# Second-choice expert rows: half the transposing loads replaced by TensorE transposes, and a reordered GpSimd queue, in a linear-attention and mixture-of-experts layer

## The chip, the cores and the metric

One Trainium2 chip, 8 NeuronCores. Each core works on one of the 8 sequences of the batch; the cores exchange nothing. The metric is the device time of the slowest core in microseconds (us). Each core has TensorE (matmul), VectorE, ScalarE, GpSimd and SyncE; SyncE and GpSimd issue the DMAs of this kernel, and 16 DMA engines carry them.

## What is computed

For every core one sequence x of 4096 tokens by 1024 features, weights shared:

```
q = elu(x Wq^T + bq) + 1;  k = elu(x Wk^T + bk) + 1;  v = x Wv^T + bv      (16 heads of 64)
attention: causal linear attention in chunks of 128 tokens, state S += k^T v, out = num / den
x1  = layernorm(x + out Wo^T + bo)
gates = softmax(x1 gate_w^T + gate_b) over 8 experts; the two largest are kept
ffn = sum over the two chosen experts e of gate_e * (x1 expert_w[e]^T + expert_b[e])
out = layernorm(x1 + ffn)
```

## The kernel before, in words

The attention runs over 32 chunks of 128 tokens in a software pipeline that is written out by hand (the loop at L771). For each chunk it ends with the first layer norm, the gate and the top-2 choice, and then `stage_scatter` (L686) sends each token's row to two lists in HBM by an indirect DMA of GpSimd: to `xs` in bf16 at its place in the list of its second choice, and to `xfd` in f32 at its place in the list of its first choice. The index of the token is stored in the row itself. Expert weights are converted to bf16 in HBM during the attention and loaded into the eight tensors W0 to W7 as these come free (`load_experts`, L752); experts 3 and 7 come last, since W3 holds Wo and W7 the attention tiles.

Each list is cut into tiles of 128 rows that belong to one expert: NT = 39 tiles. The first eight are the first tiles of the eight experts, at fixed places; the others' places and weights are read from a table (`tab`) computed after the last chunk, by register loads (`at_row` L922, `value` L911).

**Stage 1, second choices (loop at L1014).** For a tile t, `load_second` (L977) issues two DMAs on SyncE's queue: a transposing DMA that brings 128 rows of `xs` as the transposed stationary operand into one of six buffers `xTb`, and a small DMA for the 128 token indices `tk`. It is called AHEAD = 5 tiles early. `expert_mm` (L936) is 16 matmuls of 128x128 by 512 on TensorE into one of four pairs of PSUM banks. ScalarE copies the result to Y (L1022), and GpSimd scatters it to `y2d` (helper line L206). VectorE does nothing in this stage.

**Stage 2, first choices (loop at L1084).** Six tiles ahead, SyncE loads the f32 rows of `xfd` (L1001); the buffer must have been written out by the scatter to `out` (`xf_out`). Three tiles ahead, GpSimd gathers the tokens' rows of `y2d` (helper line L212). ScalarE casts the rows to bf16 (L1048), TensorE transposes them in 8 steps and the gate columns in one (L1058, L1056), ScalarE copies the transposed rows from PSUM (L1063), VectorE copies the gate columns (L1066). After two matmuls for the bias (L954) and 16 for the expert (L960), VectorE adds the gathered rows (L1107), adds the gated PSUM result (L1111), and computes mean and variance (L1117, L1121). GpSimd makes the scale and shift by three small operations, the "norm" below (L1123, L1126, L1129), ScalarE applies them (L1096) and GpSimd scatters the rows to `out` (`put_out`, L206). GpSimd's order in round t is: gather of tile t+3, output of tile t-1, norm of tile t. Every engine and each DMA queue works in the order in which the program issues.

## Time and profile before

| what | us |
|---|---|
| median of 3 runs (lowest to highest) | 1058.51 (1056.54 to 1061.42) |
| the profiled execution, whole | 1057.53 |
| its span on the slowest core, core 6 | 1056.0 |
| spans of the eight cores | 1041.1 to 1056.0 |
| PE / DVE / ACT / POOL busy on core 6 | 908.1 / 576.9 / 540.7 / 431.5 |
| HBM traffic of core 6 over the span | 227 GB/s |

The span is divided as follows on core 6: the attention until about 646 us, stage 1 from 655.72 to about 835 us, stage 2 until the end. PE is TensorE's matmul row, PEld its weight load, DVE is VectorE, ACT ScalarE, POOL GpSimd, SPq the DMA issues of SyncE. A busy share is an average over stages; what bounds a stage is read from its waits. Times in the rows below count from the first instruction of the core that they name.

### The profile page before, as it was taken

Reading aid. Unit: us, or ns where it says so; the run is one execution under the profiler, and the core shown is the slowest. Engines: PE = TensorE matmul, PEld = TensorE weight load, DVE = VectorE, ACT = ScalarE, POOL = GpSimd, SP = SyncE. Lnnn points to the kernel's source line nnn. Section 1 sums busy time; section 2 is a strip of 40 time slices with the busy share of each in tenths; the row PEclk is TensorE's granted clock in tenths of the full one; section 3 lists DMA queues with packets and bytes.
Section 4 is the critical chain, followed back from the end, with each engine's and each line's share of the span. In section 5 each row is a group of like instructions: output and inputs, shape, how many; then the busy total and the mean of one; then the engine's idle time right before and its main releaser. Section 6 shows DMA issues by size and latency. Waiting matters only on the chain.

```text
span 1056.0 us, 21222 instructions; the slowest of 8 cores (1041.1 to 1056.0 us)
## 1 busy us (share of the span) xinstructions
PE 908.1 (86%) x6495; PEld 457.0 (43%) x6606; DVE 576.9 (55%) x1243; ACT 540.7 (51%) x731; POOL 431.5 (41%) x674
## 2 busy tenths in 40 slices
PE   4799899999998999999999863579778899999992
PEld 1344454555544545554555541234333344444441
DVE  4345766766666667666667764000000088888883
ACT  0663665756657566566656541112112455666552
POOL 9101433534434334325232424313222356777763
PEclk9899999999999999999999986889989899999997
DMA  9989796977976967868537995989999768987861
GB/s 139 160 156 314 138 209 143 177 156 149 180 155 130 189 150 137 189 126 157 137 106 226 285 294 180 296 160 235 182 168 255 203 210 277 309 267 249 304 208 58
DMA packets 126490, 204.96 MB, mean 194 GB/s; under 512 B 59422, under 2 KB 73886, under 8 KB 126384
## 3 DMA queue, kind: packets, MB, share of 16 engines
q0 software_dynamic: 53808, 130.92, 54.9%
q1 hardware_dynamic: 72576, 72.69, 26.3%
q8 instruction: 59, 0.97, 0.4%
q14 instruction: 47, 0.39, 0.1%
HBM read 142.93 MB, written 97.21 MB: 227 GB/s over the span
## 4 chain that ended last, share of the span: by engine, by line
PE 52%; ACT 11%; issue 10%; DMA 8%; POOL 7%; DVE 7%; SPq 3%; DVEq 0%; ACTq 0%; POOLq 0%
PE PS L309 20%; PE PS L960 13%; PE PS L547 10%; ACT AR L325 4%; DMA AR<-xs 4%; POOL out L206 3%; ACT AR L326 3%; DMA W<-wq 2%; SPq L983 2%; PE PS L467 1%; PE PS L593 1%; PE PS L461 1%; POOL rstd L1126 1%; DMA y2d<-AR,ix 1%; PE PS L502 1%
## 5 line engine op out<-in xcount | busy, mean ns | idle before, releaser
L309 PE MATMUL PS<-W 128*128 128x512 bf16 x1474 | 347.9, 384 | 33.6 <-DVE acc L266 15.0
L960 PE MATMUL PS<-W,AR 128*128 (+1 forms) x1215 | 285.3, 391 | 46.1 <-DMA AR<-xs 40.3
L309 PEld LDWEIGHTS PS<-W 128*128 128x128 bf16 x1536 | 143.7, 99 | 192.4 <-issue 38.4
L960 PEld LDWEIGHTS PS<-W,AR 128*128 128x128 bf16 x1248 | 121.6, 100 | 208.3 <-issue 80.8
L330 DVE SCALAR_TENSOR_TENSOR W<-AR 128x512 bf16<-128x512 f32 x128 | 88.5, 692 | 140.6 <-ACT AR L326 125.3
L325 ACT ACTIVATE AR<-PS,cbs 128x512 f32<-128x512 f32 x128 | 87.9, 687 | 87.8 <-PE PS L309 82.6
L547 PE MATMUL PS<-W 128*128 128x512 bf16 x496 | 115.2, 386 | 6.5 <-DVE ixf L637 3.2
L1022 ACT ACTIVATE AR<-PS 128x1024 f32<-128x1024 f32 x39 | 39.8, 1023 | 152.2 <-PE PS L960 147.3
L1066 DVE COPY wT<-PS 16x128 bf16<-16x128 bf16 x39 | 7.3, 188 | 186.5 <-PE PS L1058 186.0
L206 POOL DMA_INDIRECT xs<-AR x32 | 34.5, 1078 | 181.4 <-DVE rden L479 143.0
L1096 ACT ACTIVATE AR<-AR,nmr,rstd 128x1024 f32<-128x1024 f32 x39 | 48.4, 1241 | 80.4 <-POOL nmr L1129 80.4
L206 POOL DMA_INDIRECT y2d<-AR,ix x39 | 37.6, 963 | 125.0 <-ACT AR L1022 110.4
L326 ACT ACTIVATE AR<-PS,cbs 128x512 f32<-128x512 f32 x128 | 87.7, 685 | 0.0
L438 DVE TENSOR_TENSOR W<-PS,cbs 128x1024 bf16<-128x1024 f32 x64 | 75.1, 1215 | 0.1
L547 PEld LDWEIGHTS PS<-W 128*128 128x128 bf16 x512 | 48.3, 99 | 60.6 <-issue 8.1
L518 ACT ACTIVATE AR<-S_f 64x520 bf16<-64x520 f32 x62 | 39.8, 642 | 51.1 <-DVE S_f L509 46.6
L206 POOL DMA_INDIRECT out<-AR x39 | 53.1, 1360 | 30.2 <-issue 9.9
L565 POOL TENSOR_TENSOR rstd<-mnv,epst 128x1 f32<-128x1 f32 x32 | 6.2, 194 | 137.5 <-DVE mnv L563 120.4
L1111 DVE SCALAR_TENSOR_TENSOR AR<-PS,AR 128x1024 f32<-128x1024 f32 x39 | 50.1, 1284 | 21.3 <-PE PS L960 20.9
L402 POOL DMA_DIRECT2D AR<-x x32 | 32.3, 1046 | 67.6 <-DMA AR<-AR 67.3
L1117 DVE BATCH_NORM_STATS2 lnst<-AR 128x6 f32<-128x512 f32 x78 | 50.2, 685 | 6.5 <-DVE AR L1111 6.2
L1107 DVE SCALAR_TENSOR_TENSOR AR<-AR 128x1024 f32<-128x1024 f32 x39 | 50.1, 1285 | 4.7 <-DMA AR<-y2d,AR 3.6
(123 smaller groups left out, 1265.4 us busy)
## 6 DMA issues: line engine op xcount, KB each, us to landing
AR<-xfd SPq DMA_DIRECT2D x39, 524.0 KB
AR<-AR SPq DMA_DIRECT2D x32, 512.0 KB, 5.8
AR<-x POOLq DMA_DIRECT2D x32, 512.0 KB, 7.2
escr<-ew POOLq DMA_DIRECT2D x64, 256.0 KB
W<-escr SPq DMA_DIRECT2D x40, 256.0 KB, 5.1
W<-xt POOLq DMA_DIRECT2D x64, 128.0 KB, 12.7
W<-escr SPq DMA_DIRECT2D x48, 128.0 KB
xfd<-AR SPq DMA_DIRECT2D x9, 524.0 KB, 6.2
```

Of the source, the lines that this page charges most:

```text
L206: return Q.op("POOL", lambda e: e.indirect_dma_start(out=out, out_offset=bass.IndirectOffsetOnAxis(ap=idx, axis=0), in_=in_, in_offset=Non ...
L309: return Q.op("PE", lambda e: e.matmul(bank(b), lt, rh, start=(k == 0), stop=(k == KB - 1)), inc="cpe" if k == KB - 1 else None)
L325: Q.op("ACT", lambda e: e.activation(e1, bank(b), AF.Exp, bias=bc), inc="cac")
L326: va = Q.op("ACT", lambda e: e.activation(e2, bank(b), AF.Relu, bias=bc), inc="cac")
L330: vd = Q.op("DVE", lambda e: e.scalar_tensor_tensor(dst, e1, 1.0, e2, ALU.min, ALU.add), inc="cdv")
L438: msc_tok[j][hf] = Q.op("DVE", lambda e, hf=hf: e.tensor_tensor(msc[j][hf].rearrange("p (h w) -> p h w", w=128), PS[:, hf * 1024:(hf + 1) ...
L547: vpe = Q.op("PE", lambda e, b=b, k=k, hh=hh: e.matmul(bank(b), attnT[j][:, k * 128:(k + 1) * 128], wcol(3, k, hh * 512, 512), start=(k == ...
L960: mm = e.matmul(bank(2 * pi + hh), xTb[i][:, k * 128:(k + 1) * 128], w, start=(lst == 1 and k == 0), stop=(k == KB - 1))
L1096: vo = Q.op("ACT", lambda e, x=x, val=val: e.activation(val, val, AF.Identity, bias=nmr[x][:, 0:1], scale=rstd[x][:, 0:1]), inc="cac")
L1107: v1 = Q.op("DVE", lambda e, i=i, j=j, val=val: e.scalar_tensor_tensor(val, Y[j], XF[i][:, F_GATE + 1:F_GATE + 2], val, ALU.mult, ALU.add) ...
L1111: v2 = Q.op("DVE", lambda e, i=i, pi=pi, val=val: e.scalar_tensor_tensor(val, PS[:, pi * 1024:(pi + 1) * 1024], XF[i][:, F_GATE:F_GATE + 1 ...
L1117: vb = Q.op("DVE", lambda e, i=i, x=x, hh=hh: e.bn_stats(lnst[x][:, hh * 6:(hh + 1) * 6], XF[i][:, hh * 512:(hh + 1) * 512]), inc="cdv")
```

## The change

1. `load_second` has two forms. For the first eight tiles and then for every even one (24 of 39) it issues one plain DMA of 128 whole rows of `xs`, the token index with them, into one of six row buffers R; no `tk` load is needed. Four of these lie in XF[6] and XF[7], two in xb. The 15 odd tiles keep the transposing DMA and the `tk` load.
2. `turn_second` transposes such a tile on TensorE (8 transposes into PSUM bank 6 or 7), and VectorE copies it to `xTb`. In round t it stands for tile t+1 ahead of the matmuls of tile t, and `load_second(t + 5)` now stands ahead of both. `expert_mm` uses three PSUM pairs, not four.
3. A plain load waits for `r_free` of its row buffer, which holds the transposes and the scatter to `y2d` of the tile before in it.
4. The weights of experts 3 and 7 (16 DMAs of 256 KB) are issued as soon as the last output projection has ended, ahead of the first five tile loads, not behind them.
5. In stage 2 the gate-column copy moves from VectorE to ScalarE, and GpSimd's order in round t becomes: norm of tile t, output of tile t-1, gather of tile t+3.
6. A row of `xs` shrinks from 1056 to 1040 elements (BW).

```diff
+    R = [XF[6 + j // 2].bitcast(BF16)[:, j % 2 * BW:(j % 2 + 1) * BW] for j in range(4)] + xb
@@ load_experts
+        if g == NCH:
+            Q.wait("SP", attnT_free[(NCH - 1) % 2])
+            for e_i in (3, 7):
+                load_w(e_i)
@@ stage 1
+    turned = lambda t: t < 8 or t % 2 == 0
+    tb, nturn = [bfree[6], bfree[7]], [0]
     def load_second(t):
-        i = ring_of(t, 1)
-        Q.wait("SP", *xT_free[i])
+        i, n = ring_of(t, 1), t % len(R)
         if t >= 8:
             Q.wait("SP", v_tab, v_padn)
+        if turned(t):
+            Q.wait("SP", *r_free[n], *(dsf if n > 3 else []))
+            r_tok[t] = Q.op("SP", lambda e: at_row(
+                e, t, 1, BW, 2, lambda rows: e.dma_start(R[n], xs[rows, :])),
+                inc=f"dr{n}", k=16)
+            return
+        Q.wait("SP", *xT_free[i])
...
+    def turn_second(t):
+        i, n, b = ring_of(t, 1), t % len(R), nturn[0] % 2
+        nturn[0] += 1
+        Q.wait("PE", r_tok[t], *tb[b])
+        for k in range(KB):
+            vpe = Q.op("PE", lambda e, k=k: e.transpose(
+                bankb(6 + b)[:, k * 128:(k + 1) * 128], R[n][:, k * 128:(k + 1) * 128], Id),
+                inc="cpe" if k == KB - 1 else None)
+        r_free[n] = [vpe]
+        Q.wait("DVE", vpe, *xT_free[i])
+        xT_tok[(t, 1)] = Q.op("DVE", lambda e: e.tensor_copy(xTb[i], bankb(6 + b)),
+                              inc="cdv")
+        tb[b] = [xT_tok[(t, 1)]]
...
     for t in range(AHEAD):
         load_second(t)
-    for e_i in (3, 7):
-        load_w(e_i)
...
+    turn_second(0)
     for t in range(NT):
-        pi, i = t % 4, t % NY
-        vpe = expert_mm(t, 1, pi)
+        pi, i, n = t % 3, t % NY, t % len(R)
         if t + AHEAD < NT:
             load_second(t + AHEAD)
         if t >= 12 and t % 4 == 0 and (t - 12) // 4 < AHEADF:
             load_first((t - 12) // 4)
+        if t + 1 < NT and turned(t + 1):
+            turn_second(t + 1)
+        vpe = expert_mm(t, 1, pi)
...
+        (r_free if turned(t) else tk_free)[n].append(y2_tok[i])
@@ stage 2
-        Q.wait("DVE", vpe, *xT_free[ring_of(t - 2, 0)])
-        wT_tok[t] = Q.op("DVE", lambda e: e.tensor_copy(
-            wT[j][:], bankb(7)[0:16, 0:128]), inc="cdv")
+        Q.wait("ACT", *xT_free[ring_of(t - 2, 0)])
+        wT_tok[t] = Q.op("ACT", lambda e: e.activation(
+            wT[j][:], bankb(7)[0:16, 0:128], AF.Copy), inc="cac")
@@ loop of stage 2, head
-        if t + 3 < NT:
-            gather_y2(t + 3)
...
-            put_out(t - 1, vo)
-        if t == NT:
+        if t == NT:
+            put_out(t - 1, vo)
             break
@@ loop of stage 2, after the norm of tile t
+        if t > 0:
+            put_out(t - 1, vo)
+        if t + 3 < NT:
+            gather_y2(t + 3)
```

## Rows read from the trace of the kernel before

**Rows 1.** Spans and mean granted TensorE clock, two of the eight cores.
```profile
core 3: 1042.0 us, clock 0.963
...
core 6: 1056.0 us, clock 0.959
```
**Rows 2.** Windows, core 6: stretch, length, busy time per engine, PEclk, DMA share, GB/s.
```profile
740.00:796.00 56.00, 41.51 (x159) 17.01 (x163) 0.00 (x0) 10.52 (x11) 13.45 (x14) 0.90 1.17 178
```
**Rows 3.** Timeline, core 6, PE, stage 1: start, length, operation, [idle before and releaser].
```profile
655.72 18.63 PE L960 MATMUL PS<-W,AR 128*128 128x512 bf16 x78 [9.34 <-DMA AR<-xs]
692.07 47.04 PE L960 MATMUL PS<-W,AR 128*128 128x512 bf16 x204 [17.71 <-DMA AR<-xs]
...
796.84 38.34 PE L960 MATMUL PS<-W,AR 128*128 x170 [0.22 <-issue]
```
**Rows 4.** Timeline, core 6: SyncE's DMA issues of the last weights.
```profile
661.80 9.22 SPq L194 DMA_DIRECT2D W<-escr  x16
```
**Rows 5.** The chain that ended last, core 6, in order of time: start, length, what.
```profile
647.86 3.60 DMA xs<-AR
...
671.06 20.73 DMA AR<-xs
...
746.61 11.19 DMA y2d<-AR,ix
```
**Rows 6.** DMA, core 6: all queues over 600 to 636, then over 636 to 652 us.
```profile
DMA packets 8106, 10.72 MB, mean 298 GB/s; under 512 B 931, under 2 KB 6358, under 8 KB 8102
...
DMA packets 1342, 3.04 MB, mean 190 GB/s; under 512 B 171, under 2 KB 768, under 8 KB 1339
```
**Rows 7.** SyncE's queue over 600-636, 692-716, 768-796 us: packets, MB, share of 16 engines.
```profile
q1 hardware_dynamic: 7256, 7.66, 73.2%
...
q1 hardware_dynamic: 8702, 1.87, 48.1%
...
q1 hardware_dynamic: 6170, 2.04, 81.8%
```
**Rows 8.** Lines L417 and L1066, core 6: copies from PSUM, duration in ns min/median/max.
```profile
L417 DVE COPY AR<-PS x32: 682/691/692, 73.5 to 617.8; 128x1024 bf16<-128x1024 bf16 x32
...
L1066 DVE COPY wT<-PS x39: 184/185/213, 838.3 to 1031.2; 16x128 bf16<-16x128 bf16 x39
```
**Rows 9.** Timeline, core 6, one round of stage 2.
```profile
855.35 0.21 DVE L1121 BATCH_NORM_AGGREGATE mnv<-lnst 128x2 f32<-128x12 f32 x1
...
855.69 1.28 DVE L1107 SCALAR_TENSOR_TENSOR AR<-AR 128x1024 f32<-128x1024 f32 x1
856.25 0.76 POOL L1123 TENSOR_TENSOR rstd<-mnv,epst 128x1 f32<-128x1 f32 x1
...
857.28 0.62 PE L1058 MATMUL PS<-id_b,AR 128*128 128x128 bf16 x8
857.37 1.28 DVE L1111 SCALAR_TENSOR_TENSOR AR<-PS,AR 128x1024 f32<-128x1024 f32 x1 [0.40 <-PE PS L960]
...
858.60 1.09 POOL L212 DMA_INDIRECT AR<-y2d,AR  x1 [0.44 <-issue]
...
860.15 0.21 DVE L1121 BATCH_NORM_AGGREGATE mnv<-lnst 128x2 f32<-128x12 f32 x1
```
**Rows 10.** Timeline, core 6, GpSimd in another round: an output that lasts longer.
```profile
914.38 2.07 POOL L206 DMA_INDIRECT out<-AR  x1 [0.31 <-DVE wT L1066]
```
**Rows 11.** Line L212 on core 3: gathers of y2d, from issue to landing.
```profile
DMA to landing us min/median/max: 2.2/7.3/9.4
```
**Rows 12.** Timeline, core 6, PE: first and last matmuls of stage 2.
```profile
841.72 1.89 PE L960 MATMUL PS<-W,AR 128*128 128x512 bf16 x4
...
1033.56 3.63 PE L960 MATMUL PS<-W,AR 128*128 x15
```
**Rows 13.** Timeline, core 3, PE: first and last matmuls of stage 2.
```profile
835.19 4.96 PE L960 MATMUL PS<-W,AR 128*128 128x512 bf16 x16
...
1020.54 3.63 PE L960 MATMUL PS<-W,AR 128*128 x16
```

More of the change, by code:

```diff
@@ L29 @@
 F_TOK, F_POS, F_GATE = 1040, 1041, 1043
-BW = 1056
+BW = 1040
 OOB = 1 << 20
@@ L111, in build @@
     attnT = [wcol(7, 6 + j, 0, 1024) for j in range(2)]
-    AR = sb("AR", [128, 18144], F32)
+    AR = sb("AR", [128, 18120], F32)
     ar_at = [0]
@@ L142, in build @@
     xb = [area(1040, BF16) for j in range(2)]
-    assert ar_end == 18144 and ar_at[0] <= ar_end - FW
+    R = [XF[6 + j // 2].bitcast(BF16)[:, j % 2 * BW:(j % 2 + 1) * BW] for j in range(4)] + xb
+    assert ar_end == 18120 and ar_at[0] <= ar_end - FW
     S_f = sb("S_f", [128, 520], F32)
@@ L975, in build @@
     tk_tok, tk_free = {}, [[] for _ in tk]
+    r_tok, r_free = {}, [[] for _ in R]
+    dsf = [Q.last(n) for n in ("dsf0", "dsf1", "dsf2", "dsf3")]
+    turned = lambda t: t < 8 or t % 2 == 0
+    tb, nturn = [bfree[6], bfree[7]], [0]
     def load_second(t):
-        i = ring_of(t, 1)
-        Q.wait("SP", *xT_free[i])
+        i, n = ring_of(t, 1), t % len(R)
         if t >= 8:
             Q.wait("SP", v_tab, v_padn)
+        if turned(t):
[5 more added lines that the diff above has]
+        Q.wait("SP", *xT_free[i])
         xT_tok[(t, 1)] = Q.op("SP", lambda e: at_row(
@@ L985, in load_second @@
             inc=f"dT{i}", k=16)
-        n = t % len(tk)
         Q.wait("SP", *tk_free[n])
@@ L997, in load_first @@
         Q.wait("SP", *fA, xf_out[i])
+        if i >= 6:
+            for j in range(4):
+                Q.wait("SP", *r_free[j])
         if t >= 8:
@@ L1024, in build @@
         pair_free[pi] = [va]
-        Q.wait("POOL", va, tk_tok[t])
-        y2_tok[i] = scatter(f"dy{i}", y2d, tk[t % len(tk)], Y[i], S - 1)
-        tk_free[t % len(tk)] = [y2_tok[i]]
+        Q.wait("POOL", va, r_tok[t] if turned(t) else tk_tok[t])
+        idx = R[n].bitcast(I32)[:, 512:513] if turned(t) else tk[n]
+        y2_tok[i] = scatter(f"dy{i}", y2d, idx, Y[i], S - 1)
+        (r_free if turned(t) else tk_free)[n].append(y2_tok[i])
         if t >= 10 and t % 3 == 1 and (t - 10) // 3 < NE:
@@ L1034, in build @@
     Q.wait("POOL", *y2_tok)
-    xb_tok, xb_free = {}, [None, None]
+    xb_tok, xb_free = {}, [r_free[4], r_free[5]]
     wT_tok = {}
-    tb_free = pair_free[3]
+    tb_free = tb[0] + tb[1]
     def gather_y2(t):
@@ L1046, in cast_first @@
         j = t % 2
-        Q.wait("ACT", xf_tok[t], xb_free[j])
+        Q.wait("ACT", xf_tok[t], *xb_free[j])
         xb_tok[t] = Q.op("ACT", lambda e: e.activation(
@@ L1060, in turn_first @@
                 inc="cpe" if k == KB - 1 else None)
-        xb_free[j] = vpe
+        xb_free[j] = [vpe]
         Q.wait("ACT", vpe, *xT_free[i])
```

## The prediction

> **What bounds the kernel now.** I read the cores first: they exchange nothing and end between 1042.0 and 1056.0 us in [rows 1] for the two that I follow, so the slowest, core 6, sets the time. Then the windows and TensorE's timeline of stage 1. Five tiles of second choices run from 655.72 us, TensorE stands still for 17.71 us, thirteen tiles run, then come gaps, and eleven tiles run again [rows 3]. The last group gives the price of a tile: 38.34 us for 11 tiles (170 of 176 matmuls are recorded) is 3.49 us. Stage 1 ends at 835.18 us, 179.5 us after its first matmul, where 39 x 3.49 = 136.1 would do. Of the 43 us too many, 17.7 are the one gap. The chain shows its cause: the sixth transposing load took 20.73 us [rows 5], because the 16 weight loads of experts 3 and 7 were issued ahead of it [rows 4]. Most of the rest lies between 740 and 796 us, where the DMA share is 1.17 at only 178 GB/s [rows 2] and the chain passes through a scatter to y2d that took 11.19 us [rows 5]: there ten tiles took 56 us, 21 more than matmuls need. So stage 1 is bound by DMA, in two places.
>
> In stage 2 the first matmuls of tile 0 and of tile 38 start 191.8 us apart on core 6 [rows 12], 5.05 us a round, and 185.4 us apart on core 3 [rows 13], 4.88 a round. A round without a delay is 4.80, from aggregate to aggregate in [rows 9]; there VectorE waits 0.40 us for TensorE and GpSimd is not late. So TensorE bounds the good rounds, and in the bad ones GpSimd's norm comes late: it stands behind an output scatter that can last 2.07 us [rows 10].
>
> **Part 1, the weights of experts 3 and 7 earlier.** This removes the 17.71 us gap whole. The new cover is the stretch from 636 to 652 us, in which the queues moved only 3.04 MB [rows 6]. At the 298 GB/s of the stretch before it [rows 6], 16 us carry 4.8 MB, so there is room for 1.7 of the 4.2 MB; the other 2.5 MB would take 8.4 us, ahead of the first tile loads in the same queue and beside the last xs scatter, which all wait for (3.60 us now, [rows 5]). The bounds are thus 0 and 8.4 us; I take 2.5, since the 3.04 MB lie in bursts with gaps between them. Tile 0 must also be turned: 0.62 us for 8 transposes [rows 9] and 0.69 for VectorE's copy [rows 8], 1.3 together. First matmul: 655.72 + 3.8 = 659.5.
>
> **Part 2, turned tiles.** TensorE gets 23 more turns inside the stage, 23 x 0.6 = 13.8 us [rows 9], all on its path. The copies are hidden: VectorE is idle there (0.00 busy, [rows 2]), and each has a whole tile's matmuls as cover; uncovered it would cost 0.7. SyncE loses 24 of 39 small index loads. For the DMA engines I compare SyncE's queue: plain weight loads 7.66 MB in 73.2% of 36 us, 290 GB/s; transposing loads 1.87 MB in 48.1% of 24 us, 162 GB/s, and in the crowded stretch 2.04 MB in 81.8% of 28 us, 89 GB/s [rows 7]. A tile of 0.27 MB so costs 0.9 us plain and 1.6 to 2.9 transposing: 0.7 to 2.0 saved for each turned one. In the crowded stretch five of ten tiles save 10 us, and TensorE itself takes 3 us more there; of the 21 us of stalls 8 would be left. The other cores show shorter gaps and I take 6 for the whole stage; bounds 0 and 21.
>
> The waits that are added: TensorE now waits for the row load of tile t+1 ahead of the matmuls of tile t, so a late load stops matmuls that could have run, and the lead shrinks from five tiles to four. SyncE waits, ahead of a plain load, for the y2d scatter of the tile six before; all later loads stand behind it. That scatter is issued some 2 us after its matmuls and lands in about 7 (a gather's median is 7.3, [rows 11]), then comes the load: about 13 us against four tiles, 15. It fits, until a scatter takes 11.19 us [rows 5]; this is why I leave the 6 us in. Three PSUM pairs suffice, as a pair is empty a tile later. The slow start of the clock stays: the first five tiles took 18.63 us, 1.2 over 5 x 3.49 [rows 3].
>
> Stage 1 so lasts 136.1 + 13.8 + 1.2 + 6 = 157.1 us and ends at 816.6, not 835.2. From there to stage 2's first expert matmul it was 6.5 us (841.72 in [rows 12]); the gate-column copy is 0.18 us on VectorE [rows 8] and I give ScalarE 0.3: 823.4.
>
> **Part 3, GpSimd's order.** The norm of tile t no longer stands behind the output of tile t-1. But its first operation meets something else: in [rows 9] L1123 starts at 856.25 and ends at 857.01, when VectorE's L1107 (855.69 to 856.97), with two inputs in SBUF, has ended. After the change VectorE starts L1107 right after the aggregate, so the norm meets it in every round. The Trainium skill, "SBUF — State Buffer", section "SBUF: two separate sides", says of the pair of SBUF ports that GpSimd shares with VectorE that it is locked for a whole instruction; this is what these two rows show. If there were no such lock, the norm would be 1.1 us earlier and rival B likelier.
>
> What the new order costs is in the gather. Before, the gather of tile T+4 was issued at 858.60, and L1107 of that tile comes three rounds after the one at 855.69, at 870.1: a lead of 11.5 us. Now the gather of T+3 follows norm T and output T-1. From the aggregate, L1123 ends after 1.66 us, and the next DMA starts 1.59 later [rows 9]; an output of 1.1 with a gap of 0.4 puts the gather at 4.75 us, 860.1, and its L1107 is due at 865.3. The lead is 5.2 us, against a landing of 7.3 in the median and 9.4 at most [rows 11]. VectorE will wait, L1107 moves back, and then the norm is no longer held: it takes about 2.2 us from the aggregate to GpSimd's next DMA. This closes a loop over three rounds: 2.2 + 1.5 until the gather starts, 7.3 until it lands, 0.1, and 4.2 from L1107 to the next aggregate (4.46 in [rows 9], less some 0.3 of waiting for TensorE): 15.3 us, or 5.1 a round, just over TensorE's 4.80. I take 5.07. The 0.19 us that VectorE saves and ScalarE gets lie off this path. Outputs move one round back as well, and with them the loads of xfd that wait for them; these have four rounds until use and stay hidden. At the end the last norm no longer stands behind an output of 1 to 2 us: 2 off the 22.4 us from the last tile's matmuls (1033.56) to the end.
>
> **The sum** on core 6, against its own span: 823.4 + 38 x 5.07 = 1016.1; + 20.4 = 1036.5, where the span was 1056.0. The execution lasted 1.5 us longer than its span, and the median is 1.0 above the profiled one: 1039.
>
> **Rivals.**
> A, the forecast: stage 1 gives 19 us, stage 2 is bound by the gather's landing and nets nothing.
> B, the gathers land in time, under 6.4 us, and the new order does what its place promises: 4.80 a round, 38 x 0.27 = 10 us less, 1029. For it: the least landing is 2.2 us [rows 11], core 3 already has 4.88. Against: the median.
> C, stalls in stage 1 stay, because half of the tiles still transpose and each load is needed a tile earlier: 21 us in the crowded stretch, not 6, makes 1054; half of it 1047. The Trainium skill, "Advanced Engine Details and Errata", section "X-Bar Transpose (TRN2)", speaks for it: it says that transposing DMAs are as fast as regular ones, so that plain loads would relieve nothing. The 162 against 290 GB/s of [rows 7] speak against it.
> D, slower than before: the gather lands later than now, as output and gather are issued back to back and the whole works closer to the DMA's limit. Stage 1 and the tail together give 19.5 us, so the point is 0.51 us a round more, 5.58, which the loop reaches at a landing of 8.8 us. At the 9.4 of [rows 11] a round is 5.8 and the time 1066.
> E, the early weights hold up the first loads by the full 8.4 us: 1045.
>
> **How the numbers follow.** A 0.45, B 0.15, C 0.17, D 0.08, E 0.15. Forecast 1039. B's 1029 with 3 less for stalls that vanish gives 1026 as the lower end; C's 1054 with the spread of the runs gives 1056. A measurement of this kernel can tell about 0.5%, 5.3 us. Faster than 1053 takes A, B, E and most of C: 0.83; within 5.3 us the rest of C and some of D: 0.11; slower 0.06.
>
> **What would show it.** In stage 1: no gap at tile 5; first matmul near 659.5; 24 turns of some 0.6 us; DMA waits of 6 us in sum, on plain loads rather than transposing ones; end near 817. In stage 2: L1107 waiting for the DMA of y2d in many rounds, first matmuls of tiles 0 and 38 some 193 us apart, L1123 rarely held. If the rounds are at 4.80 without such waits, the gather's landing was misjudged; if stage 1 keeps waits of 20 us, the relief of the queues was; if both hold and the end is late, the start was.

## The result, and the profile after

The changed kernel is slower: its median is 1075.01 us (1066.81 to 1172.35, four runs), against 1059.97 us (1056.54 to 1061.96, four runs) for the kernel before beside it. The ratio is 1.0104, with a 95% interval of 1.0068 to 1.0140, so 1.0% slower, where 1039 us was forecast and 1026 to 1056 was the range. The highest time of a kernel, here and in some runs below, comes from an execution in which one half of the chip was disturbed; the ratios leave those out, and of the changed kernel's other three the median is 1073.74 us.

The profiled execution took 1066.81 us. The page's head, and the spans of two cores:

```profile
span 1065.2 us, 21532 instructions; the slowest of 8 cores (1049.2 to 1065.2 us)
...
PE 921.5 (87%) x6684; PEld 470.2 (44%) x6798; DVE 589.1 (55%) x1228; ACT 547.7 (51%) x770; POOL 442.1 (42%) x674
...
L1140 DVE SCALAR_TENSOR_TENSOR AR<-AR 128x1024 f32<-128x1024 f32 x39 | 50.2, 1287 | 45.7 <-DMA AR<-y2d,AR 39.7
```

L1140 is the line that was L1107: VectorE adds the gathered rows. It now stands 39.7 us in waits for the gather, 18.3 of them ahead of the first tile and 21.4 in the rounds.

TensorE's timeline, stage 1 of core 0 (L1015 are the turns, L966 the expert matmuls), then the first turn of core 3:

```profile
668.23 1.86 PE L1015 MATMUL PS<-id_b,AR 128*128 128x128 bf16 x16 [20.48 <-DMA AR<-xs]
670.67 4.42 PE L966 MATMUL PS<-W,AR 128*128 128x512 bf16 x15 [0.58 <-DMA AR<-xs]
674.93 0.61 PE L1015 MATMUL PS<-id_b,AR 128*128 128x128 bf16 x8
675.37 3.62 PE L966 MATMUL PS<-W,AR 128*128 128x512 bf16 x16
678.83 0.61 PE L1015 MATMUL PS<-id_b,AR 128*128 128x128 bf16 x8
...
698.33 0.61 PE L1015 MATMUL PS<-id_b,AR 128*128 128x128 bf16 x8
698.77 7.07 PE L966 MATMUL PS<-W,AR 128*128 128x512 bf16 x32
705.68 0.61 PE L1015 MATMUL PS<-id_b,AR 128*128 128x128 bf16 x8
...
675.80 1.87 PE L1015 MATMUL PS<-id_b,AR 128*128 128x128 bf16 x16 [28.13 <-DMA AR<-xs]
```

The 17.71 us gap of [rows 3] behind tile 4 is gone, and a wait of 20 to 28 us stands ahead of tile 0. The chain of core 0 says what it is made of, an `xs` scatter of 10.27 us (3.60 in [rows 5]) and then one of the first plain loads, 9.65 (the load of tile 0 itself landed at 667.99, 8.26 us after its issue):

```profile
649.22 10.27 DMA xs<-AR
660.58 9.65 DMA AR<-xs
```

The DMA view of core 0 over 636 to 650 us, which answers to the second row of [rows 6]: in 14 us now 4.13 MB, SyncE's queue q1 with 83.7% of the engines, GpSimd's q0, in which the scatters are, with 14.6%:

```profile
DMA packets 2743, 4.13 MB, mean 295 GB/s; under 512 B 303, under 2 KB 1571, under 8 KB 2743
...
q1 hardware_dynamic: 2518, 3.29, 83.7%
q0 software_dynamic: 225, 0.84, 14.6%
...
W<-escr SPq DMA_DIRECT2D x16, 256.0 KB, 13.3
```

Over the next 10 us, 650 to 660, the weights that are left and the scatters share the engines:

```profile
q0 software_dynamic: 445, 1.56, 57.5%
q1 hardware_dynamic: 750, 1.37, 46.6%
```

The landings of the 16 weight loads, read from the trace of cores 0 to 3, say how far this went: by 652 us 4 to 7 of them had landed (1.0 to 1.8 MB), the last one landed at 665.7 to 674.9 us, and the load of tile 0 lands 0.7 to 2.3 us behind it.

The window of [rows 2], now core 0: TensorE 49.27 us busy of 56 (it was 41.51), DMA share 0.99, 215 GB/s.

```profile
740.00:796.00 56.00, 49.27 (x254) 23.68 (x257) 4.15 (x6) 12.62 (x13) 16.39 (x17) 0.94 0.99 215
```

Stage 2 of core 0: first the waits from 836 us on (us in total, times, longest; the longest, 18.3, is the wait ahead of tile 0), then the gathers' landing (L214 was L212), then two rounds.

```profile
DVE AR L1140 <- DMA AR<-y2d,AR: 39.7, 14, 18.3
...
DVE AR L1144 <- PE PS L966: 10.5, 10, 2.5
...
DMA to landing us min/median/max: 2.1/6.7/10.3
```

```profile
899.36 1.28 DVE L1140 SCALAR_TENSOR_TENSOR AR<-AR 128x1024 f32<-128x1024 f32 x1 [0.34 <-ACT AR L1098]
900.01 0.68 POOL L1156 TENSOR_TENSOR rstd<-mnv,epst 128x1 f32<-128x1 f32 x1
...
902.34 1.09 POOL L208 DMA_INDIRECT out<-AR  x1 [0.50 <-issue]
...
905.57 0.21 DVE L1154 BATCH_NORM_AGGREGATE mnv<-lnst 128x2 f32<-128x12 f32 x1
905.93 0.19 POOL L1156 TENSOR_TENSOR rstd<-mnv,epst 128x1 f32<-128x1 f32 x1 [1.16 <-DVE mnv L1154]
...
907.33 1.28 DVE L1140 SCALAR_TENSOR_TENSOR AR<-AR 128x1024 f32<-128x1024 f32 x1 [1.56 <-DMA AR<-y2d,AR]
...
907.75 1.83 POOL L208 DMA_INDIRECT out<-AR  x1 [0.48 <-issue]
...
909.89 1.03 POOL L214 DMA_INDIRECT AR<-y2d,AR  x1 [0.31 <-issue]
```

In the first of these rounds the norm's L1156 starts inside L1140 and lasts 0.68 us, until L1140 (899.36 + 1.28) is over. In the second VectorE waits 1.56 us for the gather, L1156 passes freely in 0.19, and L1140 then meets the output scatter instead, which takes 1.83 us. The gather behind it is late: 909.89 is 4.32 us after the aggregate (L1154). Such a long scatter is the rarer case: on core 0 three of the 39 last over 1.2 us.

All together, from TensorE's timelines of all cores, in us (start: first matmul of stage 1; round: from the first matmul of tile 0 to that of tile 38 of stage 2, over 38; tail: from TensorE's last matmul to the end of the span):

| | before, core 6 | after, core 0 | difference | before, 8 cores | after, 8 cores |
|---|---|---|---|---|---|
| start | 655.72 | 670.67 | +15.0 | 654.0 to 657.5 | 670.7 to 677.9 |
| stage 1 | 179.5 | 158.5 | -21.0 | 165.9 to 179.5 | 146.8 to 158.5 |
| to stage 2 | 6.5 | 7.0 | +0.4 | | |
| round | 5.048 | 5.493 | 38 x 0.445 = +16.9 | 4.88 to 5.07 | 5.36 to 5.57 |
| tail | 18.8 | 16.7 | -2.1 | 17.8 to 18.8 | 16.3 to 16.7 |
| span | 1056.0 | 1065.2 | +9.2 | 1041.1 to 1056.0 | 1049.2 to 1065.2 |

Core 0, the slowest, has the earliest start of the eight and one of the longest stages 1; in the mean of eight cores the start comes 19.1 us later and stage 1 is 21.1 us shorter. Three questions follow: why the start pays back what the gap gave, whether the turned tiles give anything, and what lengthens the rounds.

### The profile page after: what moved, and what is told of

It reads as the page before. It is cut to its first block, busy times and chain, and to the rows that moved or that the text cites. A ratio compares the mean times of both kernels' runs of the same rounds, so it can differ in the third digit from the quotient of the medians.

```text
span 1065.2 us, 21532 instructions; the slowest of 8 cores (1049.2 to 1065.2 us)
## 1 busy us (share of the span) xinstructions
PE 921.5 (87%) x6684; PEld 470.2 (44%) x6798; DVE 589.1 (55%) x1228; ACT 547.7 (51%) x770; POOL 442.1 (42%) x674
## 4 chain that ended last, share of the span: by engine, by line
PE 50%; DMA 13%; DVE 10%; ACT 10%; issue 9%; POOL 6%; DVEq 0%; SPq 0%; ACTq 0%; POOLq 0%
PE PS L311 19%; PE PS L966 12%; PE PS L549 10%; DMA AR<-y2d,AR 4%; ACT AR L327 3%; DMA AR<-xs 3%; DMA W<-xt 2%; ACT AR L328 2%; DVE lnst L1150 2%; POOL out L208 1%; PE PS L595 1%; DVE AR L1144 1%; POOL rstd L1159 1%; PE PS L469 1%; DMA y2d<-AR 1%
## 5 line engine op out<-in xcount | busy, mean ns | idle before, releaser
L966 PE MATMUL PS<-W,AR 128*128 (+1 forms) x1212 | 289.0, 394 | 5.2 <-issue 3.7
L966 PEld LDWEIGHTS PS<-W,AR 128*128 128x128 bf16 x1248 | 121.9, 101 | 162.7 <-issue 39.7
L1020 DVE COPY AR<-PS 128x1024 bf16<-128x1024 bf16 x24 | 16.6, 691 | 150.4 <-PE PS L1015 150.4
L1140 DVE SCALAR_TENSOR_TENSOR AR<-AR 128x1024 f32<-128x1024 f32 x39 | 50.2, 1287 | 45.7 <-DMA AR<-y2d,AR 39.7
L1144 DVE SCALAR_TENSOR_TENSOR AR<-PS,AR 128x1024 f32<-128x1024 f32 x39 | 50.1, 1283 | 13.6 <-PE PS L966 10.5
L208 POOL DMA_INDIRECT out<-AR x39 | 44.6, 1144 | 19.6 <-issue 19.6
L341 ACT ACTIVATE AR<-PS 128x512 bf16<-128x512 f32 x64 | 37.6, 591 | 28.3 <-PE PS L311 27.9
```

Of the source, the lines that this page charges most:

```text
L208: return Q.op("POOL", lambda e: e.indirect_dma_start(out=out, out_offset=bass.IndirectOffsetOnAxis(ap=idx, axis=0), in_=in_, in_offset=Non ...
L966: mm = e.matmul(bank(2 * pi + hh), xTb[i][:, k * 128:(k + 1) * 128], w, start=(lst == 1 and k == 0), stop=(k == KB - 1))
L1140: v1 = Q.op("DVE", lambda e, i=i, j=j, val=val: e.scalar_tensor_tensor(val, Y[j], XF[i][:, F_GATE + 1:F_GATE + 2], val, ALU.mult, ALU.add) ...
L1144: v2 = Q.op("DVE", lambda e, i=i, pi=pi, val=val: e.scalar_tensor_tensor(val, PS[:, pi * 1024:(pi + 1) * 1024], XF[i][:, F_GATE:F_GATE + 1 ...
```

## Experiments on the start: the weights of experts 3 and 7

### e4: only the early weights

```diff
@@ before.py, load_experts
+        if g == NCH:
+            Q.wait("SP", attnT_free[(NCH - 1) % 2])
+            for e_i in (3, 7):
+                load_w(e_i)
@@ stage 1, behind the first five loads
-    for e_i in (3, 7):
-        load_w(e_i)
```

> The kernel before with the weights of experts 3 and 7 issued early, nothing else. Theory: first matmul 12 to 20 us later than 654 to 657.5, no gap of 16 to 19 us at tile 5, the rest of stage 1 as before: net between 4 us faster and 4 us slower than before. Rival (the delay of the start comes from the plain loads): first matmul by 662 and the time 10 us or more below the kernel before.

Measured: 1053.94 us beside 1057.49, ratio 0.9948 (0.9907 to 0.9988). Start 663.7 to 676.5, 8 to 20 us later than on the same cores before; stage 1 146 to 156 us. The gap is gone as in the full change and comes back at the start, with no turned tile in the kernel. The start came 8 us later at least where 12 was expected; the rest is as expected. The chain of core 0, the scatter and the first transposing load:

```profile
648.38 9.62 DMA xs<-AR
...
658.23 13.19 DMA AR<-xs
```

### e3: the full change with the weights late again

```diff
@@ after.py
-            for e_i in (3, 7):
-                load_w(e_i)
@@ behind the first five loads
+    for e_i in (3, 7):
+        load_w(e_i)
```

> The changed kernel with the weights of experts 3 and 7 issued behind the first five tile loads again. Theory (the weights' depth in SyncE's queue holds back the last scatters and the first loads): the last xs scatter lands in 3.6 to 4.5 us instead of 10.3, the first expert matmul starts near 658 instead of 671 to 678, but a gap of 8 to 17 us comes back at tile 5, since its load stands behind 4 MB. Net within 6 us of the changed kernel. Rival (plain loads, the smaller row of xs or the added wait for the xfd scatters delay the start, not the weights): the first matmul stays at 670 or later.

Measured: 1062.58 us beside 1057.49, ratio 1.0041 (1.0007 to 1.0074). Start 656.0 to 661.9; the gap is back though the load of tile 5 is now plain. The chain of core 2:

```profile
664.62 21.33 DMA AR<-xs
```

TensorE stood still for 12.68 us of it. That is the longest of the eight cores: the waits of over 2 us before 712 us sum up to 0 to 12.7 us, 7.3 in the mean, where the kernel before has 15.7 to 19.3, 17.4 in the mean. Stage 1 took 153 to 170 us.

### e13: no weights of experts 3 and 7 at all

```diff
@@ after.py, load_experts
-            for e_i in (3, 7):
-                load_w(e_i)
```

> The changed kernel with the loads of the weights of experts 3 and 7 left out altogether (their tiles multiply what lies in W3 and W7). Theory (these 4.2 MB alone delay the start): the last xs scatter lands in 3.5 to 4.5 us instead of 10.3, the first expert matmul starts at 657 to 660 instead of 671 to 678, no gap follows, stage 1 lasts 147 to 152 us and ends at 805 to 812. Rival (the turned form of the first tiles, with its wait for the xfd scatters, delays the start too): first matmul at 665 or later.

Measured in a single execution: 1051.04 us (before: 1057.05). Start 656.0 to 659.8, stage 1 148 to 158 us, its end 807 to 817, rounds still 5.31 to 5.49. Where the trace has them, the last `xs` scatter lands in 2.8 to 4.6 us and a first load in 2.8 to 5.4. On four of the eight cores the start then waits for VectorE (L255 or L258, the padding rows) and no longer for DMA, as in TensorE's timeline of core 1:

```profile
654.36 1.86 PE L1011 MATMUL PS<-id_b,AR 128*128 128x128 bf16 x16 [8.20 <-DVE AR L255]
```

So the two experts' 4.2 MB are the whole delay of the start: 11 to 20 us core by core, 16.5 in the mean. At 295 GB/s 4.2 MB would take 14 us.

### e8: one expert behind the sixth, one behind the seventh load

```diff
@@ before.py, stage 1
-    for e_i in (3, 7):
-        load_w(e_i)
@@ loop of stage 1, behind load_second(t + AHEAD)
+        if t < 2:
+            load_w((3, 7)[t])
```

> The kernel before, with the weights of expert 3 issued behind the sixth tile load and those of expert 7 behind the seventh. Theory (only the order in SyncE's queue makes the gap at tile 5): first matmul at 654 to 657.5 as before, the 17.7 us gap shrinks to 0 to 5 us, and the time falls by 10 to 15 us. Rival (the DMA engines as a whole are short there, so that 4.2 MB cost their 14 us wherever they stand): the gap is spread over tiles 6 to 8 but its sum stays above 12 us, and the time falls by less than 3.

Measured: 1053.57 us beside 1056.99, ratio 0.9964 (0.9930 to 0.9997). One gap becomes two. TensorE's timeline of core 4:

```profile
685.12 5.50 PE L960 MATMUL PS<-W,AR 128*128 128x512 bf16 x16 [7.86 <-DMA AR<-xs]
700.37 39.85 PE L960 MATMUL PS<-W,AR 128*128 128x512 bf16 x171 [9.75 <-DMA AR<-xs]
```

7.86 + 9.75 = 17.61 us, the 17.71 of [rows 3] again; on core 2 it was 13.76 + 3.01. In the mean of eight cores these waits are 15.9 us (17.4 before): right behind the first loads the bytes cost their full time, wherever in the queue they stand. The rival came out, not the theory.

### e14: early weights, at most two under way

```diff
@@ e5 (below), load_experts
+            for each of the 16 weight DMAs:
+                Q.wait("SP", <the DMA two before>)
```

> The changed kernel with the gather four tiles ahead, and the early weights issued so that at most two of their 16 DMAs are under way. Theory (the scatters starve because 4 MB stand in SyncE's queue at once): the last xs scatter lands in 4 to 7 us instead of 10, while most of the weights still move in the gaps before; the first matmul is 4 us or more earlier than with the early weights unthrottled. Rival (only the bytes count, not the depth of the queue): the scatter still lands after 9 us or more, or the first loads come as late as before.

Measured: 1052.66 us beside 1057.05, ratio 0.9979 (0.9954 to 1.0004); e5, the same without the throttle, is at 0.9894. The last scatter does land sooner, in 4.3 to 6.4 us on cores 4 to 7, where the trace has it, but SyncE now stands in the waits itself, and the start is no earlier. Its timeline, core 1:

```profile
619.63 52.40 SPq L196 DMA_DIRECT2D W<-escr  x39
672.69 3.06 SPq L1002 DMA_DIRECT2D AR<-xs  x6
```

The first tile load goes out at 672.69, not at about 660; the start is at 674.7 to 680.5.

## Experiment on the turned tiles

### e12: all 39 tiles by transposing DMA

```diff
@@ e5 (below)
-    turned = lambda t: t < 8 or t % 2 == 0
+    turned = lambda t: False
-    turn_second(0)
```

> The changed kernel with the gather four tiles ahead, early weights, and no turned tile: all 39 second-choice tiles by transposing DMAs as before. Theory (a turned tile costs TensorE 0.6 us and gives back about as much in DMA stalls): stage 1 lasts 147 to 156 us from its first matmul, as with turns (146 to 156), and the time is 1045 within 4. Rival (plain loads relieve the queues, as forecast): stage 1 lasts 8 us or more longer and the time is above 1051.

Measured: ratio 0.9880 (0.9830 to 0.9929), against 0.9894 (0.9852 to 0.9936) for e5. The three times behind this ratio are 1041.88, 1045.05 and 1045.31 us; e5's median is 1045.33. Stage 1: 145 to 156 us, with turns 146 to 156. Beside the early weights the turned tiles give nothing that can be measured. TensorE's timeline of e12, core 0:

```profile
665.14 64.31 PE L966 MATMUL PS<-W,AR 128*128 128x512 bf16 x288 [18.40 <-DMA AR<-xs]
732.76 29.65 PE L966 MATMUL PS<-W,AR 128*128 x128 [3.31 <-issue]
762.57 14.22 PE L966 MATMUL PS<-W,AR 128*128 x64 [0.15 <-issue]
```

What a turn costs is the period: 3.90 us from turn to turn in the timeline of after (674.93 and the next at 678.83), where two tiles with one turn take 7.35 (698.33 to 705.68), so 3.45 for a tile and 0.45 for a turn, 10.4 us for the 23 inside the stage. What they save shows in TensorE's waits. The table has the means of eight cores for the runs with gathers four tiles ahead, e5, e12 and three that stand further below (e15, e10, e16), in us: "gap" is the sum of the waits of over 2 us before 712 us, "small waits" are all the others inside stage 1, "rest" is what is left of the stage, in which TensorE works.

| | turned tiles | weights of 3 and 7 | start | gap | small waits | rest | end of stage 1 | ratio to before |
|---|---|---|---|---|---|---|---|---|
| e15 | none | late | 657.3 | 16.5 | 11.3 | 144.8 | 829.9 | 0.9953 |
| e10 | 24 | late | 659.0 | 9.5 | 4.1 | 150.6 | 823.3 | 0.9889 |
| e12 | none | early | 670.6 | 0 | 9.6 | 140.8 | 821.0 | 0.9880 |
| e5 | 24 | early | 674.0 | 0 | 4.1 | 147.9 | 826.0 | 0.9894 |
| e16 | 24 | half early | 660.7 | 0 | 3.9 | 147.8 | 812.4 | 0.9845 |

The runs with gathers three ahead agree: small waits of 10.9 us in the kernel before, 11.5 in e4, 4.0 in e3 and 3.5 in the changed kernel. So the turned tiles do relieve the small waits, by 5.5 to 8 us beside early weights, and TensorE pays 6.5 to 7.1 for them, a little less than the 10.4 of the turns. The early weights do not relieve them. With late weights the turned tiles also shorten the gap, by 7.0 us (e15 to e10), and there they do gain: stage 1 ends 6.6 us earlier. Either part alone gives about as much as both together. The stages' ends show this better than the ratios, as the intervals of e15 (0.9924 to 0.9983) and e10 (0.9841 to 0.9936) just overlap. Two limits: a plain load also saves the small load of indices, and no run tells the two apart; and e15 lacks the other small parts of the change as well.

## Experiments on GpSimd's order

### e2: the new order alone

```diff
@@ before.py, loop of stage 2, head
-        if t + 3 < NT:
-            gather_y2(t + 3)
...
-            put_out(t - 1, vo)
@@ after the norm of tile t
+        if t > 0:
+            put_out(t - 1, vo)
+        if t + 3 < NT:
+            gather_y2(t + 3)
```

> The kernel before with GpSimd's new order alone. Theory (late gather): the loss stands alone, rounds 5.3 to 5.6 us instead of 4.88 to 5.06, stage 1 as before, time 1059 + 15 = 1074. Rival (the loss needs another part of the change, such as the copy on ScalarE or the faster stage 1): rounds stay at 5.05 and the time within 3 us of 1059.

Measured: 1066.68 us beside 1057.49, ratio 1.0101 (1.0037 to 1.0165). Start and stage 1 as before, rounds 5.23 to 5.40, tail 16.6 to 16.8. The order alone loses as much as the whole change. Waits of core 1 from 840 us on (18 waits, where the kernel before, core 0, had one in stage 2, of 5.6 us, ahead of tile 0):

```profile
DVE AR L1105 <- DMA AR<-y2d,AR: 29.8, 18, 3.8
```

### e1: the full change with the old order

e2's diff backwards, on the changed kernel; the gate-column copy stays on ScalarE.

> The changed kernel with GpSimd's order of stage 2 put back (gather of tile t+3, output of t-1, norm of t); the gate-column copy stays on ScalarE. Theory (the late gather holds VectorE): rounds return from 5.35 to 5.57 us to 4.9 to 5.05, the waits of VectorE for the y2d DMA (about 40 us) vanish, and the time falls by 38 x 0.45 = 17 us less 1 to 2 us at the end: about 1053 where the changed kernel has 1069. Rival (the copy moved to ScalarE, or loads of xfd that wait for later outputs, slow the rounds): the copy's move is still in, so if it is the cause, rounds stay above 5.3 and the time within 3 us of the changed kernel's.

Measured: 1052.31 us beside 1057.49, ratio 0.9961 (0.9943 to 0.9979). Cores 4 to 7 of its profile show a start of 669 to 673 us, stage 1 of 149 to 159, rounds of 5.07 to 5.13 and a tail of 18.8 to 18.9. The waits for the gather are gone but for the one ahead of tile 0, and most of the loss with them; that the rounds stay a little above the 4.9 to 5.05 expected, as they do on two cores of e4, is not explained.

### e5: gathers four tiles ahead

```diff
@@ after.py
-    for t in range(3):
+    for t in range(4):
         gather_y2(t)
...
-        if t + 3 < NT:
-            gather_y2(t + 3)
+        if t + 4 < NT:
+            gather_y2(t + 4)
```

> The changed kernel with the gather issued four tiles ahead instead of three, in the same place of GpSimd's new order (Y has four buffers, and the one it takes was read just before). Theory (the late gather holds VectorE): its lead grows by a whole round, from about 5 to about 10 us, over the landing of 7; the waits of VectorE for the y2d DMA fall below 5 us and the rounds to 4.8 to 4.95, so that the time is 1053 minus up to 5, against 1069 for the changed kernel. Rival (the new order is slow for another reason: outputs one round later hold back the xfd loads, or output and gather back to back crowd the queue): rounds stay at 5.3 or more.

Measured: 1045.33 us beside 1056.99, ratio 0.9894 (0.9852 to 0.9936). Rounds 4.89 to 5.03. The waits of VectorE and the landing, core 0:

```profile
DVE AR L1140 <- DMA AR<-y2d,AR: 18.4, 2, 17.7
DVE AR L1144 <- PE PS L966: 18.3, 35, 1.0
...
DMA to landing us min/median/max: 2.1/7.0/9.8
```

The gather lands no sooner (7.0 us in the median, 6.7 in the changed kernel), but it has 10.0 us from its start to its use. Of its 18.4 us of waiting 17.7 stand ahead of tile 0; in 35 rounds VectorE waits for TensorE instead, up to 1.0 us. This is the clearest evidence: only the distance was changed, and the loss (1.0104) turned into a gain (0.9894).

### e7: gather ahead of the output, still three ahead

```diff
@@ after.py, after the norm of tile t
-        if t > 0:
-            put_out(t - 1, vo)
         if t + 3 < NT:
             gather_y2(t + 3)
+        if t > 0:
+            put_out(t - 1, vo)
```

> The changed kernel with GpSimd's order norm of t, gather of t+3, output of t-1. Theory: the loop over three rounds loses the output's issue, 2.1 us and its gap of 0.3: 16.3 - 2.4 = 13.9 us, 4.65 a round, so TensorE's 4.80 should bound again and rounds come to 4.85 to 5.0; the time 15 us below the changed kernel's. Rival (the landing itself, not the issue, is what is late): the rounds fall by less than 0.2 and VectorE's waits for the gather stay above 20 us.

Measured: 1054.01 us beside 1056.99, ratio 0.9981 (0.9955 to 1.0008); rounds 5.07 to 5.29. The loop over three rounds, means of rounds 5 to 37 read off the timelines of VectorE and GpSimd:

| | aggregate to gather | gather to its add | add to aggregate | sum / 3 | round measured |
|---|---|---|---|---|---|
| after, core 0 | 4.73 | 7.46 | 4.50 | 5.56 | 5.52 |
| after, core 1 | 4.58 | 7.72 | 4.48 | 5.59 | 5.60 |
| e7, core 1 | 3.23 | 7.34 | 4.58 | 5.05 | 5.06 |
| e7, core 2 | 3.35 | 7.86 | 4.46 | 5.22 | 5.22 |
| e5, core 1 (over four) | 4.76 | 10.09 | 4.62 | 4.87 | 4.86 |

That sum and round agree is no test by itself, as the three stretches close a ring. The test is in the columns: the middle one stays at 7.3 to 7.9 us with three ahead, whatever stands ahead of the gather, and e7's 1.3 us less in the first one come back as 0.3 to 0.5 a round. Neither the 4.85 to 5.0 expected nor the rival came out: beside the wait ahead of tile 0 VectorE still waits 7.1 us for the gather on core 1 and 15.5 on core 2. In e5 the middle one grows to 10.1, over the landing, and the round is TensorE's.

### e15 and e9: what the norm ahead is worth

e15 is the kernel before with the new order and gathers four ahead; e9 is e15 with e8's edit.

```diff
@@ before.py, e2's diff with
+        if t + 4 < NT:
+            gather_y2(t + 4)
```

> The kernel before with GpSimd's new order and the gather four tiles ahead, nothing else. Theory (the order is what cost, and only by the gather's lead): rounds of 4.85 to 4.95 where the new order alone had 5.23 to 5.40 and the kernel before 4.88 to 5.07, and an end 1 to 2 us shorter: 3 to 6 us faster than the kernel before, so 1052 to 1055. Rival (norm ahead gains nothing even so): 1057 within 2.

> The weights split as in the run beside it, and in stage 2 the norm ahead of the output with the gather four tiles ahead; loads all transposing, gate-column copy on VectorE. Theory: both gains add, rounds of 4.8 to 4.9 against 4.88 to 5.06 and an end 1 to 2 us shorter: 4 to 9 us below the run with the split weights alone. Rival (norm ahead gains nothing, since the port that VectorE's first operation holds delays it anyway): the same as that run within 2 us.

Measured: e15 1051.61 us beside 1056.69, ratio 0.9953 (0.9924 to 0.9983), rounds 4.90 to 5.03, tail 16.3 to 16.7. e9 1054.76 us beside 1056.99, ratio 0.9970 (0.9932 to 1.0007), rounds 4.88 to 4.99. With enough lead the new order gains 5 us in e15 (0.2 to 0.8% by the interval), of which 1 to 2 are the tail. On top of e8's split it gains nothing: 1054.76 us against 1053.57, and the interval of e9 includes no change. What the norm ahead is worth is thus not settled; that it no longer costs 1% is.

### e11: the gate-column copy back on VectorE

```diff
@@ e5
-        wT_tok[t] = Q.op("ACT", lambda e: e.activation(
-            wT[j][:], bankb(7)[0:16, 0:128], AF.Copy), inc="cac")
+        wT_tok[t] = Q.op("DVE", lambda e: e.tensor_copy(
+            wT[j][:], bankb(7)[0:16, 0:128]), inc="cdv")
```

> The changed kernel with the gather four tiles ahead, and the gate-column copy back on VectorE. Theory (the copy's place is off the path, as forecast): rounds of 4.87 to 5.03 as without this edit, the time within 4 us. Rival (ScalarE's copy of 0.25 us ahead of the cast costs what it takes, 38 x 0.25 us): about 8 us faster.

Measured: 1047.64 us beside 1056.69, ratio 0.9925 (0.9893 to 0.9957), where e5 has 0.9894 (0.9852 to 0.9936); rounds 4.88 to 4.99. The intervals overlap and the rounds are the same: no cost of the copy's place can be told.

## Experiments for a better version

### e10: e5 with both experts late

e3's edit on e5.

> The changed kernel with the gather four tiles ahead, and the weights of experts 3 and 7 issued late, as before the change. Theory (early and late weights both cost stage 1 their transfer, early ones a little more since they also hold the last scatters): first matmul near 658, gaps of 15 to 20 us in stage 1, its end 3 to 6 us earlier than with early weights (1045 there), so about 1040. Rival (the place of the weights is neutral): 1045 within 3.

Measured: 1048.94 us beside 1057.05, ratio 0.9889 (0.9841 to 0.9936). Start 657 to 660, stage 1 158 to 170, its end 818 to 829. All early (e5) and all late cannot be told apart, and the 1040 expected did not come.

### e16: one expert early, one late

```diff
@@ e5, load_experts
-            for e_i in (3, 7):
-                load_w(e_i)
+            load_w(3)
@@ behind the first five loads
+    load_w(7)
```

> The changed kernel with the gather four tiles ahead; the weights of expert 3 early, those of expert 7 behind the first five tile loads. Theory (the delay of the start is the bytes ahead in the queue, 4.2 MB at about 300 GB/s being 14 us): half the bytes give half the delay, first matmul at 663 to 667 where all early has 666 to 679 and none 656 to 660, the rest of the weights a gap of 3 to 8 us at the sixth or seventh tile, and the same end of stage 1 (813 to 835). Rival (up to 2.1 MB fit into the pauses before the last scatters, as forecast): first matmul by 661 and no gap, the time 6 us or more faster.

Measured: 1039.84 us beside 1056.69, ratio 0.9845 (0.9802 to 0.9887), the fastest of all and faster than both kernels. Start 657.5 to 664.3, stage 1 149 to 153, its end 809 to 818, close to the 807 to 817 of e13, where these weights were never loaded. The theory missed: there is no gap, and the start is near the rival's, which is the forecast's own view of the free stretch. Rounds are 4.89 to 5.23, and on core 6 TensorE is late in them: VectorE waits for it 24.0 us in 32 waits. TensorE's timeline of core 6, its slowest core: the start, and the longest waits on the tile loads up to 757 us:

```profile
656.64 1.87 PE L1014 MATMUL PS<-id_b,AR 128*128 128x128 bf16 x16 [10.46 <-DMA AR<-xs]
659.08 4.73 PE L965 MATMUL PS<-W,AR 128*128 128x512 bf16 x15 [0.58 <-DVE AR L1019]
...
726.44 0.61 PE L1014 MATMUL PS<-id_b,AR 128*128 128x128 bf16 x8 [1.29 <-DMA AR<-xs]
```

Half of the weights, 2.1 MB, roughly fit the 1.7 MB of room that [rows 6] left before the start, and the other half the five tiles' lead behind it. On cores 0 to 3 the last early weight load lands at 654.3 to 657.9 us, before the first tile load does (658.2 to 662.0); in the changed kernel it was 665.7 to 674.9. The interval of e16 overlaps those of e5 (0.9852 to 0.9936), e10 and e12, so that it beats them is likely, by the earlier end of stage 1 (812.4 us in the mean against 821.0 to 826.0), and not certain; that it beats the kernel before is clear of the noise.

## Why the prediction was wrong, step by step

**Part 1, the weights.** Right: the 17.71 us gap goes whole (no such wait on core 0 or core 3 of the kernel after; e4). Wrong: the first matmul at 659.5, and above all the bound of 8.4 us. It came at 670.7 to 677.9, 11 to 18 us later than forecast. The step that failed is the second half of the sum, "the other 2.5 MB would take 8.4 us". The room was about right: by 652 us 1.0 to 1.8 MB of the weights had landed, for 1.7. The rest was priced at 298 GB/s, as if SyncE's queue had the engines alone. It shares them with the scatters: over 650 to 660 us it had 46.6% of them and moved 1.37 MB, GpSimd's queue 57.5% and 1.56 MB. So the other 2.4 to 3.1 MB took until 665.7 to 674.9 us, 14 to 23 us and not 8.4, with the first tile load right behind them, while the last scatter took 10.27 us instead of 3.60. e13 takes the weights away and the delay with them. e16 bears out the room: with half of the weights the start is 2.3 us later than without them, in the mean of eight cores. Rival E had this mechanism with half its size. Netted, part 1 gave 17.7 - 15.0 = 2.7 us on the cores compared, not 13.9, and in the mean of eight cores nothing: 17.4 against a start 19.1 later.

**Part 2, stage 1.** The sum came out, 157.1 us forecast and 158.5 on core 0, but not its terms, and over the eight cores (147 to 158, mean 150.9) it was 6 us too long. On core 0, 39 tiles of 3.45 are 134.6, not 136.1; the turns 10.4, not 13.8, because they overlap the matmuls behind them; the slow start 0.8 (the first tile took 4.26); and 12.7 are left for stalls, where 6 was taken: 8.3 are waits of TensorE, one of 6.43 among them, and most of the others went in matmuls at a lower granted clock around it, 0.86 over 750 to 775 us:

```profile
756.39 1.01 PE L1015 MATMUL PS<-id_b,AR 128*128 128x128 bf16 x8 [6.43 <-DMA AR<-xs]
...
750.00:775.00 25.00, 18.50 (x91) 8.98 (x94) 2.05 (x3) 5.12 (x5) 5.56 (x6) 0.86 1.04 210
```

The mechanism, that plain loads relieve the stalls, is borne out, and its size is not. The step that was mis-sized is "in the crowded stretch five of ten tiles save 10 us": TensorE's small waits fell by 5.5 us (e12 to e5) and 8.0 (e4 to the changed kernel) over the whole stage, and TensorE pays 6.5 to 7.1 for it. Two readings stand behind it. Of the 21 us too many in [rows 2] only 14.5 are idle; the others went in matmuls at a granted clock of 0.90. And the 89 GB/s of [rows 7] are not those of transposing loads alone, since the 2.04 MB hold one load of `xfd` of 524 KB. That the stage's total came out on core 0 is in part luck, as these errors offset each other. Rival C was wrong in that the stalls would stay, and near the outcome in that the turned tiles bring nothing beside early weights. The Trainium skill, "Advanced Engine Details and Errata", section "X-Bar Transpose (TRN2)", which the prediction weighed there, says that transposing DMAs are as fast as regular ones. The stage times of e12 and e5 are alike, but [rows 7] and TensorE's small waits, 9.6 us with transposing loads alone and 4.1 with 24 plain ones, do not bear it out here.

**Part 3, the rounds.** The mechanism was the right one and was written down: the gather of t+3 behind norm and output, a loop over three rounds, VectorE in waits for y2d. The landing was taken at 7.3 and was 6.7 in the median of core 0, 7.0 on core 1. Two terms were mis-sized. From the aggregate to the gather's start 3.7 us was taken, and 4.58 to 4.73 were measured; the step that failed is "L1107 moves back, and then the norm is no longer held". The text had the held value, 4.75, one sentence earlier, and dropped it. On core 0 VectorE waited for the gather in 13 rounds only, and in 25 of the 39 the norm's L1156 still runs beside L1140. The means are 0.85 us until L1156 starts and 0.59 for it, where 0.36 and 0.19 are the free values of the second round shown. Where the norm escapes the add, the output scatter can be held in its place (1.83 us against 1.09), which happened three times on core 0 and adds little to the mean. The second term, 4.2 us from the add to the next aggregate, took off the wait for TensorE; that wait stayed (10.5 us in 10 waits), and 4.5 were measured. Together 1.3 us per three rounds: 0.43 a round, 16 us over the stage. With the dropped 4.75 the forecast loop gives (4.75 + 7.3 + 0.1 + 4.2) / 3 = 5.45, 14 us more, and a forecast of 1053: the choice between two values that were both at hand cost more than any unknown.

Rival D named the outcome and the point, 5.58 a round, but tied it to a late landing of 8.8 us, which did not come; 5.36 to 5.57 a round came at 6.7 to 7.0. Rival B is refuted by e2: the new order alone has rounds of 5.23 to 5.40, not 4.80. What e5 shows, that a fourth tile of lead restores the rounds, follows from the same loop and was not among the rivals.

**Tail.** Right: 2.1 us less for 2 forecast.

**The sum.** From 1036.5 for the span to 1065.2: the start +11.2 (670.7 for 659.5), stage 1 +1.4, the way to stage 2 +0.2, the rounds 38 x 0.42 = +16.1, the tail -0.1; together 28.8 of 28.7. The errors of parts 1 and 3 have the same form: a resource that is shared, the DMA engines there and the time of GpSimd beside VectorE's add here, was priced as if it were free.

## What to carry to other kernels

Before a gather, a norm or a load is moved back in a queue, write the loop that it closes, with the contended price of every step in it, and compare lead with landing: here one tile more of lead was worth 2% and cost one number in the code. Bytes that are moved ahead of a latency-bound chain cost little as long as the free stretch carries them, and more than their own transfer once they compete with the chain's DMAs; measure with them left out how much there is to win, then move as much as the stretch carries (half of the weights early was the best of the three, though not beyond the noise). A rewrite that makes a resource cheaper by loading another one, such as turning tiles on TensorE for the DMA engines, should be tried against its own absence, with and without the other parts of the change: here it brought the end of stage 1 forward by 6.6 us beside late weights and not at all beside early ones.

## What the runs showed of the hardware that was not expected

- Sixteen plain loads of 256 KB queued on SyncE left GpSimd's indirect scatters 14.6% of the DMA engines and took their landing from 3.60 to 10.27 us; with two loads under way at most it was 4.3 to 6.4, with none 2.8 to 4.6 (after, e14, e13).
- GpSimd's issue of an indirect DMA can be stretched by VectorE's two-input add as its arithmetic is: 1.83 us against 1.09 (the round before it, at 902.34) for the same scatter. All output scatters of over 1.2 us overlap such an add (3 on core 0 and 5 on core 1 after, 20 on core 6 before); 2, 3 and 14 others overlap one and are not stretched. The Trainium skill, "SBUF — State Buffer", section "Who interferes with whom", says that such an add holds a GpSimd operation that reads SBUF, and infers that it leaves the writing of DMA descriptors alone. The scatter reads its indices from SBUF, so what was held here fits the first and does not decide the second.
- The landing of a gather was the same with three tiles of lead and with four: 6.7 and 7.0 us in the median of core 0.
- A turn of 8 transposes is recorded with 0.61 us and costs TensorE 0.45: the period of a tile with one is 3.90 us, without one 3.45.
